# V projection of the last batch in a later step, and the MLP activation evaluated twice on ScalarE in the first two layers

## The chip, the cores and the metric

One core of one Trainium2 chip runs the whole program. The metric is the time of one execution on the device in microseconds, lower is better. All times here are of this kernel and of its changed form on that chip.

## What is computed

The input is a batch of B = 4 sequences of N = 512 tokens with C = 288 channels, and a conditioning vector for each. A first layer turns the tokens by a rotation that depends on the conditioning. Then come three transformer layers, each attention and MLP, modulated by the conditioning. Cut to what matters here, with H = 16 heads of 18 channels and a hidden size of 4C = 1152:

```python
for layer in (1, 2, 3):
    h = modulate(layernorm(x), shift1, scale1)
    q, k, v = split(h @ W_qkv + b_qkv)          # layer 2 also normalizes q and k per head
    p = softmax(q @ k.T * 18 ** -0.5)           # per head, 512 x 512
    x = x + gate1 * ((p @ v) @ W_proj + b_proj)
    h = modulate(layernorm(x), shift2, scale2)
    if layer < 3:
        m = gelu(h @ W1 + b1) @ W2 + b2
    else:                                       # 4 experts, the best 2 for each token
        m = sum(g_e * (gelu(h @ W1_e + b1_e) @ W2_e + b2_e) for e in top2(router(h)))
    x = x + gate2 * m
```

Everything is fp32 to the outside.

## The kernel before, in words

**Numbers.** TensorE multiplies a rounded type (fp32r). To keep the precision, an operand is stored as a rounded high part and a rounded low part (the rest), and a product is made of three passes: high by high, low by high, high by low. For the contraction over 288 channels, packed in rows, `seven` (L2180, matmuls at L2184) needs 7 matmuls; it makes the hidden tiles of the MLP, the q and k heads ("qk" items) and V ("v" items).

**Order.** Every engine walks the same list of ticks (`ticks`, L70), written out by hand. Attention of a layer has 16 steps (4 per batch, one per group of 4 heads) of 8 ticks; the MLP has two half-ticks for each hidden tile of 128 hidden units by 512 tokens, 9 tiles (FT) per batch and 36 per layer in the first two layers, 135 in the last. In a tick an engine does its part of the main work and then the side items that `items()` (L298) put there; LAG adds ticks per engine. Engines meet only by semaphores, and each runs through its own list in order.

**Attention.** In step s, TensorE makes the scores of step s by keys (`key_scores`, L2223), which ScalarE turns into exp (L2018), and multiplies those with V (`values`, L2237); the scores by queries of step s + 2 (`query_scores`, L2205) give VectorE the row maxima (L1412). The maxima of a step are turned (L2342), brought to a row by ScalarE (L1962), and placed by SyncE's DMAs into the extra row of QK (`place_max`, L943). For batch b, the window of steps 4b to 4b + 3 also prepares batch y = b + 1: qk items (five projections, ScalarE L2005/L2006 or L2009/L2010, GpSimd L1169, then SyncE's spill to memory, L907), place items (SyncE brings two times four DMAs per step back into QK, L924 and L926; place waits for the spills and for the keys of the step that used the buffer), and v items: 7 matmuls into PSUM bank 7 (L2184), and a copy by VectorE into V (L1693). The window's ticks go on past its end: a "place" at tick 32 stands in the next window. The last window, steps 12 to 15, prepares no batch, and step 11 is the last that does: its window is the one with y = B − 1 = 3. Output projections (L2347) and transposes of q and k in layer 2 (L2327) run beside this, and the last window also loads the MLP's weights (raw<-in_w) and splits them (L1805).

**MLP.** TensorE makes hidden tile s (`hidden`, L2241), then "back" of the tile before (`back`, L2255, 12 matmuls at L2269 for 4 tiles of tokens). ScalarE takes the hidden tile out of PSUM by the gelu (`gelu_tile`, L2020). In the first two layers it writes g in fp32 (L2034) and sets f_free, by which TensorE may overwrite the bank. VectorE then casts g to the rounded G (L1773) and subtracts G from g to get the low part (L1775, g_lo). In the last layer ScalarE evaluates the gelu twice from PSUM, once to g in fp32 (L2037) and once straight to the rounded G (L2045), f_free comes after the second, and VectorE only subtracts. ROUNDED is the number of tiles of the first two layers, 72. In the first two layers all hidden tiles use PSUM bank 4, except tile 1 in bank 5; in the last layer they alternate between banks 4 and 5 (`hidden_bank`, L338). G has three buffers, g two.

Beside the MLP's tiles the side items of the layer go on: LayerNorms (ln1, ln2: L1992/L1993 on ScalarE, L1169 on GpSimd, L2323 on TensorE), scale_rows on ScalarE (L1894), output projections, and near the end of an MLP the first batch's qk, v and score items of the next layer.

The lines that the change touches are in `attention_window` (L111), in VectorE's walk (L1755 to L1775) and in `gelu_tile` (L2020 to L2045); `hidden`'s wait on f_free (L2251) keeps its meaning.

## Time and profile before

| | us |
|---|---|
| median of 3 runs | 1814.21 |
| lowest, highest run | 1813.95, 1819.57 |
| the profiled execution | 1822.59 |
| its span in the profile | 1820.8 |

Mean granted TensorE clock of the profiled execution: 0.947 of full speed.

How to read it: the time of a run is taken around the execution, the span is from the first to the last instruction in the profile of one. Every duration quoted in the prediction is from that one profiled execution, so the sum of a change is made against its time, and then carried over to the median. An engine's busy share is a mean over stages that have different limits. The chain that ended last follows the work back from the last instruction to what released it, and is the place to look for what an edit can shorten. In a timeline a bracket gives the idle time before an instruction and who ended it. PEld is TensorE's weight load, SPq SyncE's own queue. L numbers are lines of the kernel before.

### The profile page before, as it was taken

To read this page: it belongs to the slowest core of one execution; us is meant where nothing else is said; L and a number is where in the kernel's file an instruction comes from. 1 tells how busy PE (TensorE), PEld (TensorE's weight loads), DVE (VectorE), ACT (ScalarE), POOL (GpSimd) and SP (SyncE) were. 2 spreads that over 40 slices of the span, in tenths; PEclk is the share of its full clock that TensorE was granted. 3 is DMA by queue.
4 is the path that set the end of the run, shared out by engine and by line. 5 is a ranking of instruction groups with operands and counts; after the bars stand their busy time and mean duration, and the time that the engine had idled before them with its cause. 6 is when DMAs were issued, how large, how long until landed. Compare 5 with 4: busy or idle time off the path is not lost.

```text
span 1820.8 us, 28323 instructions
## 1 busy us (share of the span) xinstructions
PE 1643.5 (90%) x9431; PEld 1068.6 (59%) x9431; DVE 1227.4 (67%) x2685; ACT 1055.5 (58%) x1897; POOL 674.1 (37%) x661
## 2 busy tenths in 40 slices
PE   5876899998899897999899999999988989999997
PEld 2433444443488663444336976444435878999997
DVE  7872677775265576767733656777763776888885
ACT  2322476756546346776674533767667556777773
POOL 4431222213356332433244533223233373343442
PEclk9996799998899888999989999999999999999999
DMA  7721333223000222232310021333322445566662
GB/s 245 245 92 43 94 109 106 90 89 89 28 4 1 81 68 90 70 98 68 118 50 21 1 92 50 103 107 90 95 87 73 123 137 165 162 169 174 171 172 46
DMA packets 106768, 178.16 MB, mean 98 GB/s; under 512 B 14331, under 2 KB 61107, under 8 KB 106335
## 3 DMA queue, kind: packets, MB, share of 16 engines
q1 hardware_dynamic: 100336, 167.07, 30.1%
q0 software_dynamic: 6288, 9.29, 2.7%
q8 instruction: 76, 1.25, 0.3%
q14 instruction: 68, 0.56, 0.1%
HBM read 124.73 MB, written 51.09 MB: 97 GB/s over the span
## 4 chain that ended last, share of the span: by engine, by line
PE 62%; DVE 11%; ACT 9%; DMA 6%; issue 5%; POOL 3%; SPq 3%; ACTq 0%; DVEq 0%; POOLq 0%
PE ps L2184 21%; PE ps L2269 12%; PE ps L2237 8%; PE ps L2223 7%; PE ps L2347 6%; PE ps L2205 4%; DMA heads_t<-stage 3%; ACT Pr L2018 3%; PE ps L2323 1%; DMA raw<-in_w 1%; DVE negmax L1412 1%; DVE GT L1338 1%; PE ps L2074 1%; ACT HQ L1993 1%; SPq L924 1%
## 5 line engine op out<-in xcount | busy, mean ns | idle before, releaser
L1412 DVE TENSOR_REDUCE negmax<-ps 128x1 f32<-128x512 f32 x768 | 488.1, 680 | 219.7 <-PE ps L2205 215.8
L2018 ACT ACTIVATE Pr<-ps 128x512 f32<-128x512 f32 x768 | 410.9, 602 | 212.1 <-PE ps L2223 211.9
L2223 PE MATMUL ps<-QK 55*128 55x512 f32 x768 | 238.4, 512 | 37.3 <-ACT Pr L2018 25.8
L2269 PE MATMUL ps<-W2a,G 128*128 128x288 f32 x1512 | 230.7, 300 | 9.6 <-DVE G L1775 5.7
L2269 PEld LDWEIGHTS ps<-W2a,G 128*128 128x128 f32 x1512 | 213.8, 190 | 21.4 <-DVE G L1775 13.1
L2237 PE MATMUL ps<-Pr,V 128*32 128x512 f32 x1536 | 220.4, 648 | 0.0
L2205 PE MATMUL ps<-QK 54*128 54x512 f32 x768 | 194.8, 439 | 21.2 <-DMA QK<-HQ 7.8
L2223 PEld LDWEIGHTS ps<-QK 55*128 55x128 f32 x768 | 91.9, 190 | 201.1 <-ACT Pr L2018 107.9
L2184 PE MATMUL ps<-HQ,W1a 128*128 128x512 f32 (+3 forms) x756 | 182.0, 381 | 7.3 <-ACT g L2034 5.9
L1775 DVE TENSOR_TENSOR G<-g,G 128x512 fp32r<-128x512 f32 (+1 forms) x201 | 152.4, 763 | 40.7 <-ACT G L2045 36.4
L1169 POOL TENSOR_TENSOR HQ<-act,HQ 128x512 fp32r<-128x512 f32 (+3 forms) x72 | 93.0, 1292 | 190.2 <-ACT HQ L1993 134.2
L1169 POOL TENSOR_TENSOR stage<-act,stage 126x512 fp32r<-126x512 f32 (+1 forms) x60 | 77.3, 1288 | 204.5 <-ACT stage L2010 168.4
L2184 PEld LDWEIGHTS ps<-HQ,W1a 128*128 128x128 f32 (+1 forms) x756 | 135.7, 193 | 26.8 <-ACT g L2034 8.2
L2037 ACT ACTIVATE g<-ps,b1col 128x384 f32<-128x384 f32 (+1 forms) x135 | 82.4, 611 | 107.9 <-PE ps L2184 87.2
L2347 PE MATMUL ps<-WP,oT 128*128 128x288 f32 x384 | 123.6, 452 | 2.1 <-DVE oT L1686 2.0
L2205 PEld LDWEIGHTS ps<-QK 54*128 54x128 f32 x768 | 94.9, 195 | 46.7 <-DVE negmax L1412 22.7
L2347 PEld LDWEIGHTS ps<-WP,oT 128*128 128x128 f32 x384 | 71.2, 203 | 67.4 <-issue 34.8
L1174 POOL TENSOR_TENSOR oTok<-oTok,rsum 128x512 f32<-128x512 f32 x48 | 51.3, 1070 | 150.8 <-DVE rsum L1680 149.9
L2184 PEld LDWEIGHTS ps<-WQ,HQ 128*128 128x128 f32 (+1 forms) x560 | 81.3, 198 | 43.2 <-issue 14.4
L2184 PE MATMUL ps<-WQ,HQ 128*128 128x288 f32 (+1 forms) x560 | 99.0, 318 | 8.1 <-ACT stage L2010 3.3
L2034 ACT ACTIVATE g<-ps,b1col 128x512 f32<-128x512 f32 x72 | 49.3, 688 | 97.6 <-PE ps L2184 94.4
L1242 POOL DMA_INDIRECT out<-X,ids x33 | 65.2, 1976 | 103.2 <-DVE X L1439 86.9
(294 smaller groups left out, 2670.2 us busy)
## 6 DMA issues: line engine op xcount, KB each, us to landing
QK<-heads_t SPq DMA_DIRECT2D x192, 144.0 KB
heads_t<-stage SPq DMA_DIRECT2D x96, 252.0 KB
raw<-in_w SPq DMA_DIRECT2D x34, 576.0 KB
raw<-in_w SPq DMA_DIRECT2D x38, 432.0 KB
QK<-heads_t SPq DMA_DIRECT2D x192, 72.0 KB
tok_rows<-blank SPq DMA_DIRECT2D x4, 2700.0 KB, 20.8
XG<-tok_rows SPq DMA_DIRECT2D x11, 540.0 KB, 4.8
WP<-in_w SPq DMA_DIRECT2D x39, 144.0 KB, 3.5
```

What stands on the lines that cost most here:

```text
L1169: pool.tensor_tensor(lo[:, 0:n], act32[rows, h % 2, 0:n], hi[:, 0:n].bitcast(F32), ALU.subtract).then_inc(low_done, 1)
L1242: pool.indirect_dma_start(out_rows, bass.IndirectOffsetOnAxis(ids[:, i % 2, t:t + 1], 0), res[i % 2][:, t, :], None, compute_op=ALU.add).t ...
L1412: dve.tensor_reduce(negmax[:, m % 2, h, t:t + 1], ps[:, row_bank(l, s, i), :], AX, ALU.max, negate=True).then_inc(a_free, 1)
L1775: dve.tensor_tensor(g_at(n)[:, 1, 0:w], g32[:, n % 2, 0:w], g_at(n)[:, 0, 0:w].bitcast(F32), ALU.subtract).then_inc(g_lo, 1)
L2018: act.activation(Pr[:, t % 2, 2 * half + pair, :], ps[:, (16 * s + u) % 3, :], ACT.Exp, scale=SCALE).then_inc(b_free, 1)
L2037: act.activation(g32[:, n % 2, 0:w], bank, gelu, bias=bias)
L2184: ins = mm(o, lhs(w, h, rows[w]), rhs(w, h, rows[w]), start=p == 0, stop=p == 6)
L2205: mm(ps[:, row_bank(l, s, i), :], QK[r:r + QROW, g, 0, pair, 128 * t:128 * t + 128], QK[r:r + QROW, g, 1, pair, :], start=True, stop=True) ...
L2223: mm(ps[:, k % 3, :], QK[r:r + QROW + 1, g, 1, pair, 128 * t:128 * t + 128], QK[r:r + QROW + 1, g, 0, pair, :], start=True, stop=True).the ...
L2237: ins = mm(ps[32 * i:32 * i + 32, 6, :], V[:, s // 4 % 2, t, c:c + 32], Pr[:, t % 2, i, :], start=t == 0, stop=t == TT - 1)
L2269: ins = mm(ps[:, t, 0:C], g_at(n)[:, x, 128 * t:128 * t + 128], W2[w_ % 2][:, w, ft, :], start=ft == 0 and p == 0, stop=ft == FT - 1 and p ...
L2347: ins = mm(bank[:, 0:C], oT[:, (STEPS * l + 4 * i + g) % 5, 128 * k:128 * k + 128], WP[:, g, :], start=g == 0, stop=g == 3)
```

## The change

1. In the window that prepares the last batch (y = B − 1) the four v items stand at ticks 25, 27, 28 and 30 of the window in all layers. Before it was 1, 9, 17, 25 in layers 1 and 3 and 4, 6, 15, 22 in layer 2. Tick 25 and later are in step 11, the ticks before in steps 8 to 10.
2. In the first two layers ScalarE evaluates each gelu twice, the first time into g (fp32), the second time from the same PSUM bank into the rounded G, with f_free after the second. Ahead of the second it waits until "back" of the tile that used this G buffer is done (n < 3: no wait). VectorE's cast into G is gone. The PSUM banks of the hidden tiles stay as they are, and so does `hidden`'s wait.

```diff
--- before.py
+++ after.py
@@ -106,6 +106,10 @@
 def slot_before(n):
 
     return max([i + 1 for i in range(n) if raw_slot(i) == raw_slot(n)], default=0)
+
+
+
+VALUES = (25, 27, 28, 30)
 
 
 def attention_window(l, b):
@@ -125,14 +129,14 @@
         if l != 1:
             out += [(t, "place", l, y, g) for g, t in enumerate((8, 16, 24, 32))]
             out += [(t, "qk", l, y, j) for j, t in enumerate((2, 4, 12, 20, 22))]
-            out += [(t, "v", l, y, k) for k, t in enumerate((1, 9, 17, 25))]
+            out += [(t, "v", l, y, k) for k, t in enumerate((1, 9, 17, 25) if y < B - 1 else VALUES)]
         else:
             out += [(t, "place", l, y, g) for g, t in enumerate((11, 16, 24, 32))]
             for k, t in enumerate((1, 2, 3, 5)):
                 out += [(t, "tok", l, y, TT + k), (t + 2, "var", l, y, TT + k)]
             out += [(7, "root", l, y, 1), (9, "inverse", l, y, 1)]
             out += [(t, "qk", l, y, j) for j, t in enumerate((7, 9, 14, 17, 27))]
-            out += [(t, "v", l, y, k) for k, t in enumerate((4, 6, 15, 22))]
+            out += [(t, "v", l, y, k) for k, t in enumerate((4, 6, 15, 22) if y < B - 1 else VALUES)]
     if y2 < B:
         out += [(4 + t, "stats1", l, y2, t) for t in range(TT)]
         out += [(12 if l == 1 else 18, "mean1", l, y2, 0)]
@@ -772,8 +776,6 @@
         ALL_XS = 16 * 2 * TT * SEL
 
         FINAL = FT * (WBASE[LAYERS] - 1)
-
-        ROUNDED = FT * WBASE[LAST]
 
         def wide_of(n):
 
@@ -1769,9 +1771,6 @@
                     elif n >= 3:
                         back_done(n - 3)
                     w = wide_of(n)
-                    if n < ROUNDED:
-                        dve.tensor_copy(g_at(n)[:, 0, 0:w], g32[:, n % 2, 0:w]).then_inc(g_hi, 1)
-                        dve.wait_ge(g_hi, n + 1)
                     dve.tensor_tensor(g_at(n)[:, 1, 0:w], g32[:, n % 2, 0:w], g_at(n)[:, 0, 0:w].bitcast(F32),
                                       ALU.subtract).then_inc(g_lo, 1)
 
@@ -2030,14 +2029,13 @@
                     act.wait_ge(g_lo, n - 1)
                 gelu, bias, w = ACT.Gelu if l == 1 else ACT.Gelu_apprx_tanh, b1col[:, v % 4 if l == LAST else 0, ft:ft + 1], wide_of(n)
                 bank = ps[:, hidden_bank(l, s), 0:w]
-                if n < ROUNDED:
-                    act.activation(g32[:, n % 2, :], bank, gelu, bias=bias).then_inc(f_free, 1)
-                    return
 
                 act.activation(g32[:, n % 2, 0:w], bank, gelu, bias=bias)
                 u, at_ = divmod(n - 3, FT)
                 if n >= FINAL + 3:
                     act.wait_ge(acc_full, acc(FINAL // FT))
+                elif n < 3:
+                    pass
                 elif at_ < FT - 1:
                     act.wait_ge(g_used, (FT - 1) * u + at_ + 1)
                 else:
@@ -2248,7 +2246,7 @@
                 if s == 0:
                     pe.wait_ge(a_free, 16 * STEPS * (l + 1))
                 if n > 0 and s != 1:
-                    pe.wait_ge(f_free, n - 1 if s == EARLY or n > ROUNDED else n)
+                    pe.wait_ge(f_free, n - 1 if s == EARLY or n > FT * WBASE[LAST] else n)
                 seven(ps[:, hidden_bank(l, s), 0:wide_of(n)], lambda w, h, r: W1[w_ % 2][0:r, w, 128 * ft:128 * ft + 128],
                       lambda w, h, r: x[0:r, h, 0:wide_of(n)], KROWS).then_inc(f_full, 1)
 
```

## Rows read from the trace of the kernel before

**Rows 1.** The page, busy time by engine.

```profile
PE 1643.5 (90%) x9431; PEld 1068.6 (59%) x9431; DVE 1227.4 (67%) x2685; ACT 1055.5 (58%) x1897; POOL 674.1 (37%) x661
```

**Rows 2.** The page, the chain that ended last: share by engine.

```profile
PE 62%; DVE 11%; ACT 9%; DMA 6%; issue 5%; POOL 3%; SPq 3%; ACTq 0%; DVEq 0%; POOLq 0%
```

**Rows 3.** Stretches of attention: length, busy time of each engine, TensorE clock, DMA.

```profile
342.60:394.70 52.10, 52.10 (x286) 23.70 (x285) 37.81 (x66) 31.33 (x61) 11.71 (x12) 1.00 0.29 85
394.70:410.30 15.60, 11.54 (x73) 4.83 (x72) 12.79 (x22) 9.81 (x20) 2.33 (x2) 1.00 0.35 109
...
879.50:892.70 13.20, 12.41 (x71) 4.97 (x69) 11.30 (x20) 9.73 (x20) 2.33 (x2) 1.00 0.25 76
892.70:907.20 14.50, 9.74 (x54) 3.64 (x51) 12.01 (x22) 8.17 (x16) 1.49 (x2) 0.96 0.55 169
```

**Rows 4.** Chain, 360 to 423: start, us, work. Layer 1, steps 8 to 12.

```profile
363.05 1.12 PE ps L2184 x7
...
389.64 0.90 PE ps L2184 x3
...
391.14 0.60 ACT stage L2010
...
421.38 0.59 ACT Pr L2018
```

**Rows 5.** Timeline of TensorE, 403 to 412, layer 1, end of step 11.

```profile
406.28 0.40 PE L2205 MATMUL ps<-QK 54*128 54x512 f32 x2
410.31 0.50 PE L2223 MATMUL ps<-QK 55*128 55x512 f32 x2 [3.63 <-DMA QK<-W1a]
```

**Rows 6.** Chain, 830 to 912: start, us, work. Layer 2, steps 8 to 12.

```profile
834.21 0.46 DVE V L1693
...
906.52 0.59 ACT Pr L2018
```

**Rows 7.** Line 1773, the cast of G: durations in ns, min/median/max.

```profile
L1773 DVE CAST G<-g x72: 378/428/2587, 481.7 to 1124.8; 128x512 fp32r<-128x512 f32 x72
```

**Rows 8.** Timeline, first tile of the last layer's MLP.

```profile
1390.20 0.69 ACT L2037 ACTIVATE g<-ps,b1col 128x512 f32<-128x512 f32 x1 [0.47 <-PE ps L2237]
1390.79 0.68 ACT L2045 ACTIVATE G<-ps,b1col 128x512 fp32r<-128x512 f32 x1
...
1391.52 1.65 PE L2184 MATMUL ps<-HQ,W1a 128*128 128x512 f32 x6 [1.39 <-ACT G L2045]
```

**Rows 9.** Chain through the MLPs of layers 1 and 2: start, us, work.

```profile
480.98 0.70 ACT g L2034
...
546.79 1.63 PE ps L2269 x12
...
575.47 0.47 ACT g L2034
...
597.18 6.68 DMA heads_t<-stage
...
620.11 2.05 DVE G L1773
622.18 1.65 DVE G L1775
...
1099.42 2.52 DVE G L1773
```

**Rows 10.** Timeline, a tile of layer 1's MLP: start, us, instruction.

```profile
546.83 0.69 ACT L2034 ACTIVATE g<-ps,b1col 128x512 f32<-128x512 f32 x1 [2.53 <-PE ps L2184]
...
547.45 2.19 ACT L1894 ACTIVATE xn<-X,shift,rstd 128x288 f32<-128x288 f32 x4
...
548.12 1.48 PEld L2184 LDWEIGHTS ps<-HMv,W1a 128*128 128x128 f32 x7
```

**Rows 11.** Line 2034, the gelu: who waited for it, us and times.

```profile
  PE ps L2184: 6.1, 5
```

**Rows 12.** The MLP stretch of layer 1, columns as in rows 3.

```profile
478.50:662.10 183.60, 166.67 (x942) 139.74 (x941) 104.94 (x193) 84.60 (x130) 87.12 (x82) 0.94 0.12 37
```
## The prediction

> **What bounds the kernel now.** I read the page's busy shares first, then the chain that ended last, then the stretches around the changed steps, and last the tile pattern of the MLP. TensorE is busy 90% of the span [rows 1], and 62% of the chain is TensorE work [rows 2]. So an edit pays only where it shortens TensorE's own queue in a stretch that TensorE bounds, or fills a stretch where TensorE idles for something else.
>
> Such a pair of stretches lies around the V projection of the last batch. In layer 1, steps 8 to 10 of attention (342.60 to 394.70) have TensorE busy for all of 52.10 us, and step 11 (394.70 to 410.30) has it busy for 11.54 of 15.60: 4.06 us idle [rows 3]. The chain says why. Its last TensorE piece is the qk projection that ends at 390.54; from there it is ScalarE (391.14), GpSimd, SyncE's spill and its DMA, placements, a second spill and a weight load, down to the exp of 421.38, which ends at 421.97 [rows 4]. TensorE is not on it: it ends step 11's keys at about 406.68 and waits 3.63 us for step 12's [rows 5]. What starts before 390 moves that whole chain; what is put after it is filling. The third layer repeats this (3.33 us of idle in the place of 3.63).
>
> **Part 1: V of the last batch.** Per layer it is 4 groups of 7 matmuls, 1.12 us each on the chain (363.05 is one of them [rows 4]), and with each a V copy on VectorE (0.46 us, 834.21 [rows 6]). They move from ticks 1, 9, 17, 25 of the window (one per step 8 to 11) to 25, 27, 28, 30 (all in step 11). SyncE and GpSimd issue nothing for a V item, and no DMA is moved or passed. Only "v" itself changes its place in the walks of TensorE and VectorE. The groups share one PSUM bank, so each waits for the copy before it: 1.12 + 0.46 a group, against ticks of some 2 us (the V copy of the last batch's first group asks besides for attn V of step 7, long done); and step 12's first use, behind all of step 11, is 3 us or more after the last copy.
>
> Layers 1 and 3: three groups leave the stretch that TensorE bounds, so the chain starts 3 x 1.12 = 3.36 us sooner. The same 3.36 us enter step 11, which has 4.06 us of idle to take them. This is nearly all of the room, and the last placement also waits for step 11's last key: that key comes at about the time of now (406.3), and the placement now begins at 409.6, would begin at 406.3. I take off 0.26 for this: 3.1 us per layer, with 0 (filling costs as much as it saves) and 3.36 as its ends. Two layers: −6.2.
>
> Layer 2: the old ticks are 4, 6 (both in step 8), 15 and 22, so all four leave. The chain into step 11 starts with the qk projection at tick 27, and one group (tick 25) now lies ahead of it: 4 − 1 groups, 3.36 us, plus the hand-overs at step 8, where the V copy at 834.21 is itself on the chain (0.46 [rows 6]). The room is 0.79 us of idle in 879.50 to 892.70 and 4.76 in 892.70 to 907.20 [rows 3], most of it one wait before the exp at 906.52 [rows 6]. I take −3.7 (ends 0 and −4.6). Part 1 in sum: −9.9.
>
> **Part 2: the second evaluation, layers 1 and 2** (72 tiles; the last layer's 135 already do this). It removes a cast on VectorE, median 428 ns [rows 7], and adds an activation on ScalarE, 0.58 us behind the first (pair of the last layer: they start at 1390.20 and 1390.79 [rows 8]). f_free now comes only after it. The next hidden tile uses the same bank and waits for that: first start to TensorE's restart is 1.32 us in the pair [rows 8], where one evaluation needs about 0.72. The new waits on g_used and acc_full ask for back(n−3), which TensorE has issued before hidden(n); I cost them at nothing.
>
> Whether the 1.32 us show depends on what TensorE does meanwhile. In the steady part it does a "back" of 1.63 us between two hidden tiles (546.79 on the chain [rows 9]): gelu at 546.83, next weight load at 548.12 [rows 10], 1.29 later. So the second evaluation fits, to within 0.03 us a tile: some 30 tiles with nothing else between, 1.0 us in sum. It doesn't fit where TensorE already waits for the gelu. PE waits for L2034 5 times [rows 11], 6.1 us. The first tile of each layer (480.98) delays VectorE's work behind it by 0.59 − 0.44, and 0.58 more is paid at the next gated tile: 0.72 per layer; one more gated tile in layer 1: 0.58. And where ScalarE itself is the chain, each tile adds 0.58: 4 in layer 1 (575.47 is the first) and one in layer 2: 2.9. Layer 1's four end in a spill (597.18) and in an idle of TensorE that a DMA sets [rows 9], so they pass through. Total cost 1.0 + 1.44 + 0.58 + 2.9 = 5.9.
>
> The gain: the cast stands on the chain three times: 620.11 (2.05, and the subtract behind it 1.65), once for 0.34, and 1099.42 (2.52, and 0.69 for the subtract) [rows 9]. Without it the subtract is the one that waits for GpSimd's running operation, so of 3.70 at 620 some 2.5 stay, of 2.52 + 0.69 some 2.9: −1.2, −0.3, −0.3, and about −0.3 of VectorE delays near them: −2.1. The long instances of the cast are 2.5 us against a median of 0.43 [rows 7]; they overlap GpSimd operations. The Trainium skill ("SBUF — State Buffer", section "Who interferes with whom") says that a VectorE instruction with two SBUF inputs is blocked for the whole length of a GpSimd instruction that reads SBUF. By that rule removing the cast hands the wait to the subtract, which has two such inputs; taken as if the wait went away with the cast, part 2 would be about 4 us lower (0.69 in place of 2.5 and of 2.9). The rows cannot tell these apart, since cast and subtract always come as a pair here.
>
> Part 2: +5.9 − 2.1 = +3.8, with +1 (only the tiles on ScalarE's chain pay) and +7 as its ends; beyond that is a rival.
>
> **Sum.** −9.9 + 3.8 = −6.1. The profiled execution took 1822.59 us (span 1820.8), the median of the three runs is 1814.21, 0.5% below it, and one of the three was 1819.57: the terms are the same, only the base differs. For the granted clock I add −0.6: it was 0.96 in 892.70 to 907.20, the stretch with the long idle, against 1.00 in those before it [rows 3], 0.04 x 14.50 us, and part 1 closes that idle; part 2 opens small ones, in stretches at 0.94 [rows 12], so this is no more than a guess at the sign. 1814.2 − 6.1 − 0.6 = 1807.5.
>
> **The rivals.**
> (a) *Step 11 is the bound once it is full.* 3.36 us go into 4.06 of idle; if V groups land between keys and delay the last key and with it the placement, most comes back. For: the last TensorE piece before the idle ends only some 3 us before the placement that it also releases [rows 5]. Against: the idle is one piece behind all keys, so groups ahead of it push keys only into time that is free. Then part 1 gives −2 to −3 in all: 1814.2 − 2.5 + 3.8 = 1815.5.
> (b) *Part 2 costs nearly nothing and VectorE's relief counts* (the wait for GpSimd goes with the cast, 4 us; and half of the gated tiles are covered by the DMA behind them, 597.18 [rows 9], 2 us). Then part 2 is 3.8 − 6 = −2: 1814.2 − 9.9 − 2 = 1802.3. Against: a subtract with its operands ready still meets the same GpSimd operation.
> (c) *The one bank gates TensorE in every tile: slower.* In place: L2251 behind L2034's pair. It decides once the first evaluation starts more than about 0.3 us after hidden's end (1.63 − 1.32); now it starts 0.04 after it in the steady part, but later where LayerNorm and scale work of ScalarE stands ahead. At 0.5 us on half of the 72 tiles it is +18, with part 1 −9.9: 1822. For: scale work of 2.19 us runs on ScalarE right behind that gelu (547.45 [rows 10]), and the pair delays it. Against: ScalarE is half idle there (84.60 of 183.60 busy [rows 12]).
> (d) *It doesn't do what it says*: the rounded second evaluation is not faster to G than cast plus subtract. G complete is then start + 0.59 + 0.68 + 0.69 against 0.70 + 0.44 + 0.69, +0.13. Nobody waits for G that closely, so this shifts nothing by itself; within (a)'s range.
>
> **How the numbers follow.** A measurement of this kernel can tell about 0.3%, 5.4 us: faster is below 1808.8, slower above 1819.6. Chances: forecast (1804 to 1811) 0.46; (a), with (d), (1811 to 1817) 0.23; (b) (1798 to 1804) 0.20; (c) (above 1817) 0.11. Of the forecast's 0.46 about 0.33 lie below 1808.8. So faster 0.33 + 0.20 = 0.53; same 0.13 + 0.23 + 0.01 = 0.37; slower 0.10. The range 1799.5 to 1817 leaves out the far end of (b) and (c). Its low end is near the sum with part 1 at −4.6 − 6.72, part 2 at −2 and the clock's share (1800.3); its high end is part 1 at nearly nothing (−1) with part 2 at its 3.8.
>
> **What would show it.** Right: TensorE's idle before step 12's first key shrinks from 3.63 to under 1 us in layers 1 and 3; steps 8 to 10 are 3.4 us shorter, step 11 about as long as now; PE's waits for L2034's line grow by 5 to 8 us, in few places; the steady tile stays at 3.2 us. Wrong on part 1: the idle at step 12 is gone, but step 11 is longer by 3. Wrong on part 2: the tile pattern grows from 3.2 to over 3.4 us, or TensorE's waits for the gelu come 30 times and more. A clock lower by a hundredth over one of the MLP stretches would be some 1.7 us, and would cover either.

## The result, and the profile after

| kernel | runs | median us | lowest, highest | ratio to before, 95% interval |
|---|---|---|---|---|
| changed, first comparison | 6 | 1823.9 | 1819.98, 1828.31 | 1.0054 [1.0031, 1.0077] |
| before, beside it | 6 | 1814.08 | 1812.15, 1819.57 | |
| changed, second comparison | 12 | 1826.84 | 1819.92, 1831.82 | 1.0014 [0.9990, 1.0038] |
| before, beside it | 17 | 1821.3 | 1815.08, 1835.6 | |

The change brings no gain. In the first comparison it is slower, by 9.8 us. In the second the ratio is 1.0014 and its interval includes 1, so by itself it shows no difference. Both medians lie above the predicted range of 1799.5 to 1817. (The ratios are those of the record; they are not exactly the quotients of the two medians, which would be 1.0030 in the second comparison.) A run over 1.5% above the fastest of its kernel, which is one of v_all's 12 below, is left out of its ratio. The kernel before spreads more than its first three runs showed: 35 runs beside a later group had 1811.68 to 1831.09, median 1820.95. So the first comparison may overstate the loss. What decides below are the traces: most stretches repeat within 0.1 us from kernel to kernel where the granted clock is the same. Where it is not, the text gives it: 1.00 is TensorE at 2.4 GHz, and a lower mean is a stretch that ran in part at the other level, 1.2 GHz. The profiled execution of the changed kernel took 1822.13 us, its span is 1820.4.

The page's busy times, as [rows 1] had them. VectorE has 54 us less to do, ScalarE 39 more, and TensorE's share of the span (90%) and of the chain (62%) is what it was:

```profile
PE 1645.6 (90%) x9431; PEld 1071.4 (59%) x9431; DVE 1173.2 (64%) x2613; ACT 1094.4 (60%) x1969; POOL 673.1 (37%) x661
```

The same windows in the changed kernel and in the kernel before (length, busy time of PE, PEld, DVE, ACT, POOL, TensorE clock, DMA share, GB/s): steps 8 to 10 of layer 1, step 11, the MLP of layer 1, the MLP of layer 2. A step is counted here from its first exp to the next step's first exp. First the changed kernel, then before:

```profile
340.10:392.60 52.50, 51.39 (x273) 21.69 (x272) 37.46 (x65) 31.51 (x63) 11.47 (x11) 1.00 0.29 87
392.60:406.90 14.30, 13.85 (x91) 7.39 (x84) 11.77 (x22) 8.65 (x18) 2.32 (x2) 1.00 0.34 111
471.00:657.50 186.50, 166.43 (x943) 140.31 (x941) 78.28 (x157) 103.95 (x166) 87.16 (x83) 0.95 0.12 36
964.00:1128.90 164.90, 157.53 (x872) 130.56 (x870) 69.33 (x131) 90.18 (x145) 67.16 (x57) 0.98 0.11 35
```

```profile
343.30:395.90 52.60, 52.60 (x294) 23.74 (x292) 38.47 (x68) 31.76 (x63) 11.45 (x11) 1.00 0.29 86
395.90:410.80 14.90, 10.83 (x72) 4.69 (x64) 11.59 (x20) 8.68 (x18) 2.33 (x2) 1.00 0.36 110
479.20:662.60 183.40, 166.46 (x942) 139.48 (x941) 104.94 (x193) 83.90 (x128) 87.60 (x83) 0.94 0.12 37
967.00:1130.40 163.40, 155.81 (x872) 129.21 (x870) 97.58 (x167) 69.98 (x109) 67.98 (x57) 0.99 0.12 36
```

Steps 8 to 10 have lost three V groups (294 matmul records before, 273 now, 7 fewer for each group) and are 0.2 us shorter (52.4 us after 52.6, from exp to exp; the windows round this). TensorE, busy for all of 52.60 us before, has 1.1 us of idle in them. Step 11 took the V work into its idle time as forecast (10.83 of 14.90 busy, now 13.85 of 14.30). The MLPs are 3.1 and 1.5 us longer. The idle before step 12 is closed, as the prediction said (3.63 in [rows 5]), and a wait a little later is longer:

```profile
406.39 0.71 PE L2221 MATMUL ps<-QK 55*128 55x512 f32 x2 [0.23 <-DMA QK<-W1a]
...
418.21 0.79 PE L2221 MATMUL ps<-QK 55*128 55x512 f32 x1 [1.61 <-ACT Pr L2017]
```

That second wait was 1.11 us before (TensorE, at 422.01). Counted from the start of step 8, TensorE goes on behind it at 78.1 us instead of 78.7. So up to this point part 1 gave 0.6 to 0.7 us in layer 1. It did not last to the end of step 12. Here is step 12 of layer 1, in the changed kernel and then before:

```profile
406.90:426.40 19.50, 17.16 (x76) 6.85 (x74) 14.13 (x26) 9.73 (x19) 3.69 (x2) 0.82 0.46 138
```

```profile
410.80:427.20 16.40, 15.07 (x77) 5.82 (x73) 13.35 (x24) 9.68 (x18) 3.69 (x2) 0.90 0.53 159
```

In both kernels TensorE's clock fell to 1.2 GHz behind an idle stretch: before, 67.8 us after the start of step 8, behind the 3.63 us; in the changed kernel at 78.1 us, behind the second wait. In layer 3 of the changed kernel step 12 stayed at clock 1.00, and took 16.7 us where it took 15.8 before at 0.91. Steps 8 to 12 together took 86.3 us in layer 1 (before 83.9) and 83.5 in layer 3 (before 83.3).

### The profile page after: what moved, and what is told of

Same layout as the page of the kernel before. It is cut to its first block, busy times and chain, and to the rows that moved or that the text cites. A ratio compares the mean times of both kernels' runs of the same rounds, so it can differ in the third digit from the quotient of the medians.

```text
span 1820.4 us, 28323 instructions
## 1 busy us (share of the span) xinstructions
PE 1645.6 (90%) x9431; PEld 1071.4 (59%) x9431; DVE 1173.2 (64%) x2613; ACT 1094.4 (60%) x1969; POOL 673.1 (37%) x661
## 4 chain that ended last, share of the span: by engine, by line
PE 62%; DVE 12%; ACT 9%; issue 6%; DMA 5%; POOL 5%; SPq 2%; ACTq 0%; DVEq 0%; POOLq 0%
PE ps L2182 20%; PE ps L2267 11%; PE ps L2235 8%; PE ps L2221 7%; PE ps L2345 6%; PE ps L2203 5%; ACT Pr L2017 3%; DMA heads_t<-stage 2%; DVE negmax L1414 2%; PE ps L2321 2%; DMA raw<-in_w 1%; ACT HQ L1992 1%; DVE GT L1340 1%; ACT act L1991 1%; POOL tok_rows L1233 1%
## 5 line engine op out<-in xcount | busy, mean ns | idle before, releaser
L2033 ACT ACTIVATE g<-ps,b1col 128x512 f32<-128x512 f32 (+1 forms) x207 | 131.7, 636 | 191.0 <-PE ps L2182 163.8
L2203 PE MATMUL ps<-QK 54*128 54x512 f32 x768 | 200.6, 445 | 18.3 <-DVE negmax L1414 7.7
L2043 ACT ACTIVATE G<-ps,b1col 128x512 fp32r<-128x512 f32 (+1 forms) x201 | 127.0, 632 | 0.0
```

What stands on the lines that cost most here:

```text
L2033: act.activation(g32[:, n % 2, 0:w], bank, gelu, bias=bias)
L2043: act.activation(g_at(n)[:, 0, 0:w], bank, gelu, bias=bias).then_inc(f_free, 1)
L2203: mm(ps[:, row_bank(l, s, i), :], QK[r:r + QROW, g, 0, pair, 128 * t:128 * t + 128], QK[r:r + QROW, g, 1, pair, :], start=True, stop=True) ...
```

## The experiments

Ticks that changed are given by the diff; L numbers move by a few lines between kernels, so lines are named by their work.

### The two parts alone

**v_all**, **v_13** and **v_2** are the kernel before with V of the last batch moved in all layers, in layers 1 and 3, and in layer 2. **g_two** is the changed kernel with V at its old ticks.

```diff
-            out += [(t, "v", l, y, k) for k, t in enumerate((1, 9, 17, 25))]
+            out += [(t, "v", l, y, k) for k, t in enumerate((1, 9, 17, 25) if y < B - 1 else VALUES)]
```

(v_13; v_2 has the same in the other branch; g_two has only the rest of the change.)

> Only part 1 of the change (V of the last batch at ticks 25, 27, 28, 30, all layers), one evaluation with VectorE's cast as before. Theory C (covered): at their old place the V groups filled time in which TensorE would wait for VectorE's row maxima and ScalarE's exp, so steps 8 to 10 stay within 1 us of their length in each layer, and layer 2 loses 3 to 5 us in step 11, where the groups queue behind a bank that ScalarE frees: +3 to +6 us in all. Theory P (the prediction's, with only part 2 mis-sized): steps 8 to 10 get 3.4 us shorter, -8 to -10 us in all.

> V moved in layers 1 and 3 only, nothing else changed. Theory C (covered): no more than 1 us gained per layer, so -2 to 0 us in all, unless TensorE's clock falls at another place. Theory P: -6 us.

> V moved in layer 2 only. Theory C: step 11 of layer 2 is 4 to 6 us longer, the steps before 1.5 us shorter, +2 to +5 us in all. Theory P: -3.7 us. If the loss of step 11 is only an effect of the double evaluation or of chance, this run shows step 11 at 13 to 15 us.

> Only part 2 (double evaluation in the first two layers, one bank), V at its old ticks. Prediction's ledger: +3.8 us (1 to 7), with the MLP of layer 1 2.9 and of layer 2 0.9 us longer. Rival (one bank gates TensorE at each tile): +10 to +18. If the whole change is the sum of its parts, this and the run with all V groups moved add up to +9.8.

| kernel | ratio (12 runs each, 35 of before) | layer 1: steps 8, 9, 10, 11 | MLP 1 | MLP 2 |
|---|---|---|---|---|
| before | | 17.7, 17.3, 17.5, 15.0 | 183.4 | 163.4 |
| v_all | 1.0001 [0.9975, 1.0027] | 17.7, 17.1, 17.6, 14.6 | 183.9 | 161.7 |
| v_13 | 0.9998 [0.9979, 1.0017] | 17.7, 17.1, 17.6, 14.3 | 182.3 | 163.0 |
| v_2 | 1.0014 [0.9988, 1.0040] | 17.7, 17.3, 17.5, 14.9 | 183.6 | 163.1 |
| g_two | 1.0013 [0.9989, 1.0036] | 17.7, 17.3, 17.6, 15.1 | 186.6 | 164.9 |

(Lengths in us, from one trace each.) The forecast's −9.9 us for part 1 would be a ratio of 0.9946; v_all's interval excludes it. v_13 has steps 8 to 10 at 52.4 us against 52.6. The +3 to +6 us that I expected of v_all did not show in its time either: its ratio is 1, and the interval ends at +4.9 us.

Nor does V's move gain anything up to the end of step 12 in layers 1 and 3. Eight readings with V moved to 25, 27, 28 and 30 (v_13, v_all, both traces of the changed kernel) have 83.5 to 86.5 us for steps 8 to 12; ten with V in place (before, v_2, g_two, and g_banks and g_tail below) have 83.3 to 85.5. Over steps 8 to 14 it is 117.2 to 121.6 and 117.0 to 120.6. How much of the 0.7 us goes to the place of the clock's fall and how much to the longer second wait, these traces do not separate.

g_two's cost sits in the MLPs, as the ledger (the prediction's sum of costs and gains) had it: 2.7 to 4.3 us in layer 1 against the four traces without part 2 in this table, 1.5 to 3.2 in layer 2. Part of that is clock, as the section on part 2 shows. In its whole time it does not show: the interval of g_two's ratio includes 1.

### The whole once more

> The changed kernel once more, beside more runs of the kernel before. The parts gave ratios of 1.0001 (V) and 1.0013 (double evaluation), the first runs of the whole 1.0054. If the whole is the sum of its parts, 1.001 to 1.003, some +2 to +5 us; if the two parts disturb each other, 1.004 to 1.007 again, and then some step is longer here than in either part alone.

1.0014 [0.9990, 1.0038] agrees with the sum of the parts (0.01% and 0.13%, each with about 0.25% of uncertainty). Its steps 8 to 10 of layer 1 are 17.7, 17.1 and 17.6, its MLPs 184.9 and 165.2 us: nothing in it stands out beside the parts.

### Layer 2: where the freed steps went

Steps 8 to 10, step 11 and step 12 of layer 2 as three windows, in v_2 and then before:

```profile
822.20:882.00 59.80, 54.04 (x273) 23.93 (x271) 40.52 (x78) 38.84 (x71) 20.82 (x25) 0.89 0.26 81
882.00:899.70 17.70, 15.57 (x98) 8.27 (x97) 13.02 (x24) 10.00 (x20) 2.34 (x2) 1.00 0.23 69
899.70:914.10 14.40, 12.28 (x66) 4.74 (x66) 13.17 (x24) 9.63 (x20) 3.69 (x2) 0.95 0.53 158
```

```profile
822.20:880.40 58.20, 54.77 (x299) 26.35 (x298) 41.99 (x82) 38.80 (x70) 20.84 (x25) 0.94 0.28 84
880.40:893.60 13.20, 12.43 (x70) 4.98 (x70) 11.28 (x20) 9.73 (x20) 2.33 (x2) 1.00 0.26 81
893.60:912.00 18.40, 13.85 (x66) 5.19 (x66) 13.19 (x25) 9.66 (x20) 3.68 (x2) 0.84 0.50 152
```

Step 11 grew from 13.2 to 17.7 us, about the four groups (4 x 1.12). Step 12 shrank from 18.4 to 14.4, at clock 0.95 instead of 0.84: of the 3.83 us that TensorE waited there for an exp behind a weight load, 1.42 are left, the rest is hidden by that work now. The steps before gave little: in the traces where the clock was 1.00 in step 10 it took 16.1 to 16.3 us instead of 16.7, and step 8 went from 19.4 to 18.9. In all, steps 8 to 12 took 91.9 us here, 91.8 in v_all and 92.4 and 90.7 in the two traces of the changed kernel, against 89.8, 91.0, 91.2 and 90.9 in four traces with V at its old place (before, v_13, g_two, turn_old). All 15 traces with V at its old place in layer 2 lie between 88.8 and 92.2: no gain, where −3.7 was forecast. TensorE also meets a new wait in step 11 (changed kernel, timeline of TensorE):

```profile
880.54 1.20 PE L2182 MATMUL ps<-WQ,HQ 128*128 128x288 f32 x7 [1.69 <-ACT stage L2005]
```

The V group of tick 27 stands right behind the q/k item of tick 27 in the same PSUM bank, and ScalarE empties that bank late. **v2_ticks** moves the groups away from it, in layer 2 alone:

```diff
-            out += [(t, "v", l, y, k) for k, t in enumerate((4, 6, 15, 22))]
+            out += [(t, "v", l, y, k) for k, t in enumerate((4, 6, 15, 22) if y < B - 1 else (25, 26, 29, 30))]
```

> Layer 2 alone moved, with its V groups at ticks 25, 26, 29, 30 in place of 25, 27, 28, 30: none of them directly behind the q/k item of tick 27, whose bank ScalarE frees late. If that bank wait is a cause of step 11's growth, TensorE's wait of 1.69 us before the second V group is gone and step 11 takes 15.5 to 16.5 us in place of 17.8; if the growth is only the 4.5 us of V work, it stays at 17.5 to 18.

Step 11 took 15.9 us and the bank wait is gone, as expected. It is not a gain: TensorE then waits 3.0 us in step 12 for the exp behind the weight load, where v_2 waited 1.4. Steps 11 and 12 together are 33.4 us, against 32.1 in v_2 (with TensorE's clock at 0.84 in step 12 here and 0.95 there, so one trace each cannot say what the bank wait alone is worth).

### What took the place of the V groups

In v_13, VectorE at the start of step 8, where the first V group was:

```profile
341.41 1.29 DVE L1415 TENSOR_REDUCE negmax<-ps 128x1 f32<-128x512 f32 x2 [0.87 <-PE ps L2208]
342.61 0.70 DVE L1689 STREAM_TRANSPOSE oT<-oTok 128x512 f32<-128x512 f32 x1
343.24 1.25 DVE L1415 TENSOR_REDUCE negmax<-ps 128x1 f32<-128x512 f32 x2
344.41 0.70 DVE L1681 STREAM_TRANSPOSE oTok<-ps 128x512 f32<-128x512 f32 x1
345.14 0.25 DVE L1683 RECIPROCAL rsum<-oTok 128x16 f32<-128x16 f32 x1
345.31 2.42 DVE L1415 TENSOR_REDUCE negmax<-ps 128x1 f32<-128x512 f32 x4
```

From 341.41 to 347.73 VectorE works without a gap: row maxima, the turn of one step's output, maxima, the transpose and reciprocal of the next, maxima. TensorE's score matmuls need the banks that these maxima free. The chain of the kernel before was TensorE's work alone through all three steps, up to 390.54. That of the changed kernel has this run of VectorE on it in step 8, one wait for an exp in step 9, the run of VectorE again in step 10 (373.40 to 378.34), and then the qk group from which the spills start:

```profile
343.63 0.56 DVE negmax L1414
...
359.75 0.59 ACT Pr L2017
...
373.40 1.19 DVE negmax L1414 x2
...
377.78 0.56 DVE negmax L1414
...
386.34 0.90 PE ps L2182 x3
```

The q/k group ends at 387.24, 47.1 us after the start of step 8; before it was at 390.54 [rows 4], 47.3 us after it. The chain that the prediction wanted to start 3.36 us earlier starts 0.2 us earlier. **turn_old** and **turn_moved** move one of VectorE's items out of that crowd, without and with V moved:

```diff
-            out += [(8 * g + 1, "out", l, s - 1, 0), (8 * g + (3 if g == 0 else 7), "turn", l, s - 1, 0)]
+            out += [(8 * g + 1, "out", l, s - 1, 0), (8 * g + (3 if g == 0 else 4 if l != 1 and b in (1, 2) else 7), "turn", l, s - 1, 0)]
```

> V at its old ticks; in layers 1 and 3, windows of batches 1 and 2, VectorE's transpose of the attention output (0.70 us) moved from tick 7 of a step to tick 4, away from the ticks where it stands beside six row maxima and the turn of the output. Theory C (TensorE and VectorE bound steps 8 to 10 alike): TensorE is still full there with its V groups, so each of steps 8 to 10 stays within 0.3 us of 17.7, 17.3 and 17.5. Rival (VectorE alone bounds them, TensorE's matmuls only look full): each gets 0.5 to 0.7 us shorter.

> The same move of VectorE's transpose, with V of the last batch at ticks 25, 27, 28, 30 in layers 1 and 3. Theory C: with both relieved, each of steps 8 to 10 gets 0.5 to 0.7 us shorter than the 17.7, 17.1 and 17.6 it has with V moved alone. Rival (something third, as ScalarE's exps or the DMA of the placements, bounds them): no step changes by more than 0.2.

**v_dup** issues each V group of the last batch twice in layers 1 and 3, at the old ticks:

```diff
+                        if kind == "v" and l != 1 and i == B - 1:
+                            seven(bank[:, 0:C], lambda w, h, r: x[0:r, h, 128 * t:128 * t + 128],
+                                  lambda w, h, r: WQ[0:r, w, c:c + C], QROWK)
```

> The kernel before, with the 7 matmuls of each V group of the last batch issued twice in layers 1 and 3, at the old ticks (the first set is overwritten, so nothing else changes). Taking the groups away left steps 8 to 10 at 17.7, 17.1, 17.6 us against 17.7, 17.3, 17.5. Theory C (two bounds of the same length meet in these steps): adding work shows in full although taking it away shows nothing, so each of steps 8 to 10 is 0.9 to 1.2 us longer. Rival (TensorE is not a bound there at all, its 17.7 of 17.7 busy only looks full): 0 to 0.3 us longer.

**exp_old** and **exp_moved** are turn_old and turn_moved with half exps in steps 8 to 10:

```diff
+                w = 256 if l != 1 and 8 <= s <= 10 else 512
-                act.activation(Pr[:, t % 2, 2 * half + pair, :], ps[:, (16 * s + u) % 3, :], ACT.Exp, scale=SCALE).then_inc(b_free, 1)
+                act.activation(Pr[:, t % 2, 2 * half + pair, 0:w], ps[:, (16 * s + u) % 3, 0:w], ACT.Exp, scale=SCALE).then_inc(b_free, 1)
```

> V at its old ticks, VectorE's transpose at tick 4, and in steps 8 to 10 of layers 1 and 3 ScalarE's exp over only the first 256 of 512 columns (this leaves out half of the exps there, the matmuls stay as they are). Theory C: TensorE is a bound of its own, so steps 8 to 10 stay within 0.3 us of the 17.6, 17.3 and 17.5 they have with full exps. Rival (ScalarE or VectorE alone bound them): 1 us shorter or more each.

> The same half exps and the same transpose, with V of the last batch moved in layers 1 and 3 to 25, 27, 28, 30. Theory C: what took the place of the V groups is the wait for exps (three banks of scores) and for row maxima; with both shortened each of steps 8 to 10 gets 0.7 to 1.1 us shorter than with V at its old ticks (17.6, 17.3, 17.5), about the 1.12 us of a V group. Rival (the time went into something that neither feeds, as issue or weight loads on TensorE): no more than 0.3 us shorter than 16.7, 17.1, 17.3.

**out_moved**, **both_moved** and **both_old** cut VectorE's first transpose as well (both: with half exps). These five kernels leave out work that the result needs. They serve only to show how long the steps are without it, and their whole times are not compared:

```diff
+                    if l != 1 and 7 <= i <= 9:
+                        dve.transpose(oTok[:, 0:1, :].rearrange("p c e -> p (c e)"), ps[:, 6, 0:32]).then_inc(o_out, 1)
+                    else:
...
```

> V moved in layers 1 and 3, VectorE's second transpose at tick 4, full exps; and the first transpose of the attention output (0.63 us, at tick 1 of steps 8 to 10, the tick that the V group has left) cut to 32 of 512 columns (this leaves out most of that transpose for steps 7 to 9 of layers 1 and 3). If VectorE's work in tick 1 alone holds these steps, they get 0.5 us shorter or more than 16.7, 17.1, 17.3. If ScalarE's exps hold them just as long, no more than 0.2.

> As the run before, and with exps of 256 of 512 columns in steps 8 to 10. Half exps alone left step 9 at 17.1 with VectorE's transpose on the chain. If VectorE's tick 1 and ScalarE's exps together took the place of the V groups, each of steps 8 to 10 is now 0.5 to 0.9 us shorter than 17.2, 17.1, 17.3. If something third holds them, they stay within 0.2.

> The same two cuts (half exps, short first transpose) with V at its old ticks. If TensorE is a bound of its own with the V groups in place, steps 8 to 10 stay at 17.5, 17.3, 17.6 within 0.3; else they fall as in the run before.

| V groups | VectorE, ScalarE | steps 8, 9, 10, layer 1 | layer 3 |
|---|---|---|---|
| twice (v_dup) | as before | 18.5, 18.3, 18.5 | 18.5, 18.3, 18.5 |
| once (before) | as before | 17.7, 17.3, 17.5 | 17.8, 17.3, 17.6 |
| once | turn at tick 4 (turn_old) | 17.6, 17.3, 17.5 | 17.6, 17.3, 17.6 |
| once | and half exps (exp_old) | 17.5, 17.3, 17.6 | 17.5, 17.3, 17.6 |
| once | and short transpose (both_old) | 17.6, 17.3, 17.6 | 17.6, 17.3, 17.6 |
| none (v_13) | as before | 17.7, 17.1, 17.6 | 17.7, 17.1, 17.6 |
| none | turn at tick 4 (turn_moved) | 16.7, 17.1, 17.3 | 17.2, 17.1, 17.3 |
| none | and half exps (exp_moved) | 17.2, 17.1, 17.3 | 17.1, 17.1, 17.3 |
| none | and short transpose, full exps (out_moved) | 17.0, 16.8, 17.1 | 17.1, 16.8, 17.0 |
| none | all three (both_moved) | 17.1, 16.8, 17.0 | 17.0, 16.8, 17.1 |

(Lengths in us, one trace each, all at clock 1.00. turn_moved's 16.7 is no gain: its step 7 is 1.0 us longer, 15.4 for 14.4.) The first of v_dup's three steps; TensorE is busy for all of each:

```profile
341.00:359.40 18.40, 18.40 (x104) 8.87 (x102) 13.51 (x24) 10.88 (x22) 3.62 (x3) 1.00 0.32 91
```

Read downward, the table has a kink at one V group. With V in place, no relief of VectorE or ScalarE shortens a step by more than 0.2 us: TensorE is a bound. A doubled group costs 0.8 to 1.0 us. But the first group of 1.12 us is worth only 0 to 0.2: right below TensorE's time lies a second bound. Its parts come off in small bits: the turn gives 0 to 0.5, the transpose another 0 to 0.3, and shorter exps nothing, alone or on top, which refutes the part of my expectation that named them. My expectations for the kernels with V moved were too high throughout: 0.5 to 0.7 us a step for turn_moved (it got 0 to 0.5), 0.7 to 1.1 for exp_moved (0.2 to 0.4 against V in place), 0.5 or more for out_moved and 0.5 to 0.9 for both_moved (0 to 0.3 each against the kernel they build on, that 16.7 left aside). exp_moved's chain shows what was left on it in step 9, VectorE's maxima, transpose and reciprocal, and only then TensorE:

```profile
362.48 0.64 DVE oTok L1681
...
363.14 0.25 DVE rsum L1683
363.39 0.56 DVE negmax L1415
...
363.99 0.50 PE ps L2209
```

With everything cut (both_moved) the steps are 0.5 to 0.8 us shorter than with V, half of a group or a little more, and the chain there is TensorE alone. Its weight loads in the tick that lost its V group show where the rest is:

```profile
359.69 0.19 PEld L2230 LDWEIGHTS ps<-QK 55*128 55x128 f32 x2
359.80 0.19 PEld L2212 LDWEIGHTS ps<-QK 54*128 54x128 f32 x2
360.04 0.19 PEld L2230 LDWEIGHTS ps<-QK 55*128 55x128 f32 x1
360.66 0.18 PEld L2230 LDWEIGHTS ps<-QK 55*128 55x128 f32 x1 [0.44 <-ACT Pr L2025]
...
361.20 0.18 PEld L2212 LDWEIGHTS ps<-QK 54*128 54x128 f32 x1 [0.25 <-DVE negmax L1415]
```

Two score matmuls on the two halves of the rows normally start together (359.69 and 359.80, x2). In the tick that follows without other work between, the second of each pair waits: 0.44 us for an exp that frees one of the three score banks (at 360.66), and 0.25 for a row maximum (361.20). The 7 matmuls of V stood in that gap, between the two pairs (in the kernel before from 362.98 to 364.17, with the next pair starting together at 364.10). How much a fourth score bank would give was not tried.

### Where the placement waits

```diff
-            out += [(t, "v", l, y, k) for k, t in enumerate((1, 9, 17, 25))]
+            out += [(t, "v", l, y, k) for k, t in enumerate((1, 9, 17, 25) if y < B - 1 else (25, 28, 31, 31))]
```

> Layers 1 and 3 only: V of the last batch at ticks 25, 28, 31, 31, so that two groups come after step 11's last keys. With the changed kernel's ticks the placement into step 11's rows started at 406.04 behind the last key, 1.7 us after the second spill had landed. If that is where the freed idle time went, the placement starts 1 to 1.7 us sooner after step 11's start, and steps 11 and 12 together are 0.7 to 1.7 us shorter than with V at 25, 27, 28, 30 (at the same clock). If the weight load behind it sets the time alone, nothing changes.

The placement starts 65.9 us after the start of step 8 (404.67 − 338.8), as with the changed ticks (406.04 − 340.1 = 65.9), against 66.3 before (409.60 − 343.3). Steps 11 and 12 took 31.0 us (the clock at 1.00 throughout), where they took 31.1 in layer 3 of the changed kernel at the same clock. Two groups after the last keys instead of ahead of them change nothing, so the keys don't set the placement, and my reading of the 1.7 us fell. What does set it was not tested. A candidate that fits is the spill, which hangs on the q/k group that did not move.

### Part 2: bank, ScalarE and VectorE

Chain of the changed kernel through the tiles that [rows 9] showed from 575.47 on, and after it the steady tile of [rows 10]:

```profile
567.20 0.47 ACT g L2033
...
567.78 0.68 ACT G L2043
```

```profile
538.51 0.69 ACT L2033 ACTIVATE g<-ps,b1col 128x512 f32<-128x512 f32 x1 [1.99 <-PE ps L2182]
...
539.10 0.68 ACT L2043 ACTIVATE G<-ps,b1col 128x512 fp32r<-128x512 f32 x1
...
539.83 1.46 PEld L2182 LDWEIGHTS ps<-HMv,W1a 128*128 128x128 f32 x7
```

Where ScalarE is the chain, the second evaluation adds its 0.68 us less the overlap: gelu starts 5.78, 5.51, 5.51 and 4.98 us apart in tiles 23 to 26, against 5.21, 4.94, 4.93 and 4.40 before, so +0.57 or +0.58 each, 2.3 in sum. In the steady tile the weight load follows the gelu's start by 1.32 us, and a bare tile takes 3.26 instead of 3.22 us. TensorE's waits for ScalarE's evaluations in the two layers stay at 5 and grow from 6.1 [rows 11] to 7.5 us.

Where the double evaluation costs and where it gives shows best in pairs of traces with the same mean clock over the MLP. Stretches from gelu to gelu, in us:

| MLP, kernel, clock | tiles 0 to 7 | 7 to 23 | 23 to 27 | 27 to 35 | 35 to the next layer's first exp |
|---|---|---|---|---|---|
| layer 1, one evaluation (v_13), 0.96 | 33.8 | 59.5 | 19.5 | 54.6 | 13.2 |
| layer 1, two (after_again), 0.96 | 34.1 | 60.3 | 21.8 | 54.6 | 12.4 |
| layer 2, one (v_dup), 0.98 | 29.4 | 63.0 | 23.7 | 40.6 | 6.3 |
| layer 2, two (after_again), 0.98 | 29.8 | 63.3 | 24.3 | 39.7 | 6.3 |

That is +2.6 us in layer 1 and +0.4 in layer 2 (g_two's trace gives +0.1 there), or about +3 in all. The rest of g_two's +4.2 to +7.5 goes with a lower clock: where the four traces have 33.7 to 35.0 us in tiles 0 to 7 of layer 1, the long end is at clock 0.90, as g_two's 35.2 is, and the short end at 0.95. The lower clock in tiles 23 to 27 of layer 2, worth 1.5 us, is in all three traces with the double evaluation in one bank, but also in 3 of the 14 with one evaluation; whether the change brings it about stays open.

**g_banks** gives the double evaluation a second bank, **g_tail** keeps it (in one bank) only for tiles 27 to 35:

```diff
-    ahead = l == LAST
+    ahead = l == LAST or s < 22
...
-                    pe.wait_ge(f_free, n - 1 if s == EARLY or n > FT * WBASE[LAST] else n)
+                    pe.wait_ge(f_free, n - 1 if 2 <= s <= 22 or n > FT * WBASE[LAST] else n)
```

```diff
+        def single(n):
+            return n < ROUNDED and n % (4 * FT) < 3 * FT
...
-                if n < ROUNDED:
+                if single(n):
```

> Double evaluation in the first two layers as in the changed kernel, but with the hidden tiles alternating between two PSUM banks up to tile 22, as the last layer does; V at its old ticks. If the one bank is what part 2 pays for (prediction's rival c), the MLP of layer 1 falls from 186.6 back to 183.5 us or less and that of layer 2 from 165.0 to 163. Ledger: only the steady tiles (3.26 in place of 3.22) and the first gated ones depend on the bank, so layer 1 gets 0.5 to 1.2 us back of 3.1 and tiles 23 to 26, where ScalarE's own work is the chain, keep their 0.58 each.

> Double evaluation only in tiles 27 to 35 of layers 1 and 2, where VectorE works on the next layer's row maxima; one evaluation and VectorE's cast in tiles 0 to 26; V at its old ticks. Ledger: the 0.58 per tile where ScalarE is the chain are gone, and what VectorE's relief gives is left: layer 1 -0.5 to +0.5 us, layer 2 -0.5 to -1.5. Rival (VectorE's relief gives nothing, the extra evaluation costs everywhere alike): +0.7 us or more in each layer.

g_tail: from the gelu of tile 27 to that of tile 35 it is 39.8 us in layer 2 (before 40.7, at the same clock of 0.96): −0.9. In layer 1 it is 53.6 (before 54.5), but at clock 0.94 for 0.87, and v_dup, which has one evaluation, also took 53.6 there, at 0.90. What is clear in layer 1 is the stretch behind tile 35: 12.4 or 12.5 us in all six traces with the double evaluation there, 13.2 at clock 1.00 without it. So VectorE's relief is real and small, 0.8 and 0.9 us. g_banks: 178.7 and 162.5 us for the two MLPs, 7.9 and 2.4 less than g_two, far more than the ledger's 0.5 to 1.2. By these two numbers alone the bank's branch of my expectation was met, but not for its reason. Tiles 23 to 26 kept their 0.58 each, as expected. Most of the gain is at tiles 3 and 4, and it has little to do with the second evaluation. With one bank and one evaluation (v_13), the gelu of tile 3 stands behind ScalarE's scale work, and TensorE waits for it:

```profile
484.33 2.17 ACT L1897 ACTIVATE xn<-X,shift,rstd 128x288 f32<-128x288 f32 x4
...
486.85 0.67 ACT L2037 ACTIVATE g<-ps,b1col 128x512 f32<-128x512 f32 x1
...
487.57 2.78 PE L2187 MATMUL ps<-HQ,W1a 128*128 128x512 f32 x7 [3.55 <-ACT g L2037]
```

With two banks (best, the last kernel, below) TensorE makes the next hidden tile while ScalarE scales, and both gelus follow together:

```profile
482.14 1.78 PE L2191 MATMUL ps<-HQ,W1a 128*128 128x512 f32 x7
482.60 2.17 ACT L1901 ACTIVATE xn<-X,shift,rstd 128x288 f32<-128x288 f32 x4
...
485.12 1.25 ACT L2041 ACTIVATE g<-ps,b1col 128x512 f32<-128x512 f32 x2
```

From the first gelu to that of tile 7 it is 33.8 us in v_13 and 28.5 with two banks:

```profile
474.60:508.40 33.80, 29.47 (x148) 24.48 (x149) 14.98 (x28) 13.27 (x20) 17.01 (x17) 0.95 0.05 15
```

```profile
472.90:501.40 28.50, 27.76 (x148) 23.38 (x149) 14.89 (x28) 13.20 (x21) 17.07 (x17) 1.00 0.06 18
```

Of the 5.3 us, 3.55 are the stall. TensorE's busy time is 1.7 us less for the same matmuls: the clock fell right behind the stall in v_13 and did not fall with two banks. The stall is in the kernel before too, whose gelu of tile 3 starts at 493.19.

What became of the cast that waited for GpSimd (2.05 us, and 1.65 for the subtract [rows 9])? g_two at that place:

```profile
613.14 2.66 POOL L1269 TENSOR_TENSOR X<-X,rowt 128x1152 f32<-128x1152 f32 x1
...
614.34 2.03 DVE L1774 TENSOR_TENSOR G<-g,G 128x512 fp32r<-128x512 f32 x1
```

The subtract took 2.03 us, from 614.34 to 616.37, while GpSimd's X operation of 2.66 us ran from 613.14 to 615.80; it ended 0.57 us after it. So the wait passed to the subtract. The Trainium skill's "SBUF — State Buffer", section "Who interferes with whom", has it so for a VectorE instruction with two SBUF inputs beside a GpSimd instruction that reads SBUF, and this trace agrees. The block lasts until the GpSimd instruction that began first is done, and not for its whole length, as the prediction put the rule. In the kernel before, the cast ran beside GpSimd's X operation (619.20 to 621.87) and the subtract beside the next one (621.94 to 623.28). This second wait is gone, since the pair is one instruction now: 1.67 us less on VectorE. At the place of 1099.42 in layer 2 [rows 9], 2.52 and 0.69 us, g_two's subtract alone took 2.85.

### A version that beats both

**best** is the kernel before with two banks up to tile 22, the double evaluation only in tiles 27 to 35, V moved in layers 1 and 3, and the turn at tick 4 there (the diffs above, together).

> What the runs left standing, put together: hidden tiles of layers 1 and 2 in two banks up to tile 22, double evaluation only in tiles 27 to 35 (one evaluation and the cast before), V of the last batch moved in layers 1 and 3 alone, and VectorE's transpose at tick 4 there. By the traces: the MLP of layer 1 falls from 182.3 to 183.4 to 176 or 177 us (178.7 with two banks, less 4 x 0.58), that of layer 2 from 163.0 to 161.5, the V move with the transpose gives 0.9 in layer 1 and 1.2 in layer 3: -8 to -11 us in all, ratio 0.994 to 0.9955. Rival (two banks only let TensorE run ahead into the same DMA and VectorE waits, and 178.7 was a matter of where the clock fell): -2 to -4 us, ratio 0.998 to 0.999.

8 runs, median 1805.73 us, beside 13 of before with 1821.9: ratio 0.9923 [0.9897, 0.9949]. Its MLP stretches:

```profile
471.10:646.10 175.00, 161.26 (x943) 136.46 (x941) 99.19 (x184) 88.69 (x138) 88.27 (x83) 0.98 0.13 38
945.20:1106.70 161.50, 155.42 (x871) 129.50 (x869) 93.83 (x158) 75.15 (x118) 67.86 (x57) 0.99 0.11 36
```

175.0 and 161.5 us, 8.4 and 1.9 less than before. The ratio is −14 us [−18.8, −9.3], beyond the far end of my −8 to −11, though the interval reaches into it. Clock has a part in it: the mean granted clock in the MLP of layer 1 is 0.98 here and 0.94 before, and over the whole runs it is 0.960 in the 8 and 0.952 in the 13 beside them. That less idle is what kept the clock up was not tested. What the moved V and the turn contribute was not measured apart in this kernel; by the table above it is 1 us or so up to step 10 in each of the two layers. Two banks alone, with one evaluation, were not measured either.

## Why the prediction was wrong, point by point

- **Part 1, layers 1 and 3 (−3.1 each).** Wrong, and this is the step that decided. "Three groups leave the stretch that TensorE bounds, so the chain starts 3 x 1.12 = 3.36 us sooner": it started 0.2 us sooner. I took TensorE's 52.10 busy of 52.10 [rows 3] as proof that its work is all that counts. It proves only that adding costs (v_dup: +0.8 to +1.0), not that removing gains. The 1.12 us on the chain per group was there because the group was the last to end in its tick; close behind it, so that a whole group gained 0 to 0.2 us a step, ended VectorE's maxima and the turnaround of the score banks. The low end that I gave (0 per layer) came true by luck: I had put it down to the filling of step 11, rival (a), while the saving was lost in steps 8 to 10. Measured: 0.7 us in each layer up to the wait in step 12, and nothing clear of the spread by the end of step 12.
- **Step 11 as filling, and the idle before step 12.** Right: 4.06 us of idle took 3.36 us of V, and 3.63 fell to 0.23.
- **Part 1, layer 2 (−3.7).** Wrong by the same step. Here four groups really lengthened step 11 (+4.5) and hid a weight load's wait in step 12 (−4.0, part of it clock), with about 1 us from the steps before where the clock held; in sum nothing clear of 1 us.
- **The one bank wait of V.** I counted on groups waiting only for the copy before them. One of them waits 1.69 us for a q/k item's bank, behind which it was put. Taking this wait away showed no gain, in one trace at a lower clock.
- **Part 2 (+3.8, ends +1 and +7).** The mechanism was right, and the size near: about +3 at equal clock, +4.2 to +7.5 with the clock of g_two's trace. The costs are 4.7 us where the ledger had 5.9, the gains 1.7 where it had 2.1. The four tiles at 0.58 were met to 0.01 us. The sign that I gave for it, TensorE's waits for the gelu's line longer by 5 to 8 us, was wrong: they grew by 1.4. The cost sits on ScalarE's own chain, where TensorE waits for other things. Rival (c), that the bank gates every tile, is refuted for the steady part: 3.22 to 3.26 us a tile.
- **The hand-over of the cast's wait for GpSimd.** Right: 2.03 us for the subtract where the cast had 2.05, and 2.85 in layer 2 where I had 2.9.
- **The base.** 1814.2 was the median of three runs that lay low; later groups of the same kernel have medians of 1820.95, 1821.3 and 1821.9. The sum from the profiled execution (1822.59) would have been the better base. The sign would have been wrong all the same, and in the first comparison, whose base is 1814.08, this does not explain the miss.
- **The clock's −0.6.** A guess, and no run speaks for it: v_2 hides that idle in layer 2 and has 0.89 in steps 8 to 10, where before has 0.94, and step 12 of the changed kernel has 0.82 in layer 1 and 1.00 in layer 3.

With the measured terms, at equal clock, part 2 is about +3 us, layers 1 and 3 are −1.4 to 0, and layer 2 is −1 to +1. That makes +0.6 to +4 us, a ratio of 1.000 to 1.002, and up to +8.5 with the clock of g_two's trace. The second comparison (1.0014) lies in it. The first (1.0054 [1.0031, 1.0077], +5.6 to +14 us) lies above it, and no step of the traces accounts for the difference. Which of the two is nearer stays open.

## What to carry to other kernels

An engine that is busy for all of a stretch, with its work on the chain, tells what added work costs and not what removed work gains: before counting a saving, ask which wait would end next in each tick, and look for filler work between two instructions that share banks. The cheap test is to double the work and to take it away: if the doubling shows and the taking away does not, a second bound lies right below. And before adding work to an engine that releases a buffer, look whether the buffer itself is what its partner waits for: in these traces the second bank gave more (6 us in layer 1's MLP up to tile 7, clock included) than the double evaluation cost.

## What was not expected

- Filler work is nearly free in the right place: the same 7 matmuls cost 0 to 0.2 us in a tick between two pairs of score matmuls, and 0.8 to 1.0 us when doubled there.
- The kernel before ran between 1811.16 and 1835.6 us in the 71 runs of the four groups. Over 35 of them, time and mean granted clock go together, but loosely: 0.962 at 1811.68, 0.950 at 1831.09, and 0.948 at 1820.05. Most stretches at full clock repeat within 0.1 us from trace to trace.
- One second bank for tiles 3 and 4 removed a stall of 3.55 us of TensorE and shortened the start of layer 1's MLP by 5.3 us, the rest being clock.
